# ScalarE's copy of the turned probabilities is moved ahead of the exponential in the even steps of a two-layer attention kernel

## The reference, cut to what matters

```
x   = x + attention0(queries = layernorm(x), keys = values = ctx)   # causal, 16 heads of 64
x   = x + ffn0(layernorm(x))             # gate and up 128 -> 352, down; inputs and weights rounded to FP4
x   = x + attention1(layernorm(x), ctx)  # two softmaxes: 77 text keys, 51 image keys, summed
out = x + moe1(layernorm(x))             # router, 2 of 8 experts, 128 -> 512 -> 128
# attention, per head: softmax(q k^T / 8) v, heads joined, times Wo
```

## Time and profile before

| | |
|---|---|
| median of 3 runs | 696.55 us (695.96 to 699.38) |
| the profiled execution, its own time | 694.58 us |
| its span, first to last instruction | 692.8 us |
| granted TensorE clock, mean | 0.984 |
| busy: TensorE matmul / VectorE / ScalarE / GpSimd | 625.9 / 530.0 / 439.0 / 296.2 us |

### The profile page before, as it was taken

How to read it: one execution, slowest core, us unless ns; L and a number is a source line. 1 busy time by engine, 2 the same in 40 slices (tenths; PEclk the granted TensorE clock), 3 DMA queues, 4 the chain that set the end, 5 groups by cost and what they waited for, 6 DMA issues and landing times.

```text
span 692.8 us, 16579 instructions
## 1 busy us (share of the span) xinstructions
PE 625.9 (90%) x5849; PEld 569.7 (82%) x5849; DVE 530.0 (76%) x1454; ACT 439.0 (63%) x1121; POOL 296.2 (43%) x428
## 2 busy tenths in 40 slices
PE   3779999999899989999999999999999998979980
PEld 2668888888888878999998989988988887979980
DVE  7896677788898888979889898697757675665655
ACT  3668787877777686556565655556656555656660
POOL 3143444334434343353434343334328565565550
PEclk9999999999999999999999999999999999999995
DMA  9700000000000000206666122000000001212215
GB/s 230 229 0 2 1 3 1 1 3 1 1 2 1 1 18 1 89 35 123 124 123 124 29 78 75 2 1 1 3 1 28 28 25 44 62 55 63 73 52 185
DMA packets 49389, 33.27 MB, mean 48 GB/s; under 512 B 9414, under 2 KB 45868, under 8 KB 49308
## 3 DMA queue, kind: packets, MB, share of 16 engines
q1 hardware_dynamic: 47036, 27.55, 16.7%
q0 software_dynamic: 2272, 4.67, 2.0%
HBM read 17.57 MB, written 14.63 MB: 46 GB/s over the span
## 4 chain that ended last, share of the span: by engine, by line
PE 54%; DVE 15%; issue 12%; ACT 9%; POOL 7%; DMA 2%; another core or an unknown queue 0%; POOLq 0%; SPq 0%; ACTq 0%; DVEq 0%
PE ps_s L569 6%; PE ps_j L402 6%; PE ps_h L641 5%; PE ph L1472 5%; PE ps_t L605 5%; PE ps_j L364 4%; ACT scores L782 4%; PE ps_h L620 4%; PE py L1483 4%; PE ps_j L366 4%; PE ps_j L365 3%; DVE scores L1047 3%; POOL probs L1309 3%; POOL xs_scratch L1401 3%; DVE neg_max L1054 2%
## 5 line engine op out<-in xcount | busy, mean ns | idle before, releaser
L1309 POOL TENSOR_TENSOR probs<-scores,rsums 128x308 f32<-128x308 f32 (+1 forms) x192 | 152.8, 810 | 229.6 <-DVE rsums L1067 228.6
L1062 DVE TENSOR_REDUCE sums<-scores 128x4 f32<-128x308 f32 (+1 forms) x192 | 90.8, 500 | 40.1 <-ACT scores L782 34.8
L605 PE MATMUL ps_t<-ident,probs 128*128 128x128 f32 x512 | 78.8, 276 | 21.6 <-ACT probsT L796 18.5
L782 ACT ACTIVATE scores<-scores,neg_max 128x128 f32<-128x128 f32 x256 | 81.6, 393 | 20.2 <-DVE neg_max L1054 19.9
L669 ACT ACTIVATE QT<-ps_j 128x512 f32<-128x512 f32 x64 | 38.3, 598 | 79.6 <-PE ps_j L366 79.5
L605 PEld LDWEIGHTS ps_t<-ident,probs 128*128 128x128 f32 x512 | 57.9, 141 | 28.4 <-issue 23.0
L796 ACT ACTIVATE probsT<-ps_t 128x512 f32<-128x512 f32 x128 | 75.3, 589 | 5.8 <-PE ps_t L605 5.8
L569 PE MATMUL ps_s<-KT,QT 64*128 64x128 f32 x1024 | 75.3, 287 | 0.8 <-ACT KT L675 0.8
L620 PE MATMUL ps_h<-probsT,V 128*64 128x128 f32 x1024 | 70.0, 279 | 0.9 <-DVE x_sb L827 0.8
L569 PEld LDWEIGHTS ps_s<-KT,QT 64*128 64x128 f32 x1024 | 63.0, 189 | 8.9 <-issue 2.4
L641 PE MATMUL ps_h<-Wo,headsT 128*128 128x128 f32 x512 | 69.1, 278 | 0.0
(11 more groups left out here) (239 smaller groups left out, 1608.7 us busy)
## 6 DMA issues: line engine op xcount, KB each, us to landing
xs_scratch<-xs SPq DMA_DIRECT2D x8, 1032.0 KB, 8.1
xt<-xs_scratch SPq DMA_DIRECT2D x39, 64.5 KB
w1b<-in_L_ffn_w_dram SPq DMA_DIRECT2D x1, 2048.0 KB, 9.5
big_raw<-in_L_ffn_w_dram SPq DMA_DIRECT2D x8, 256.0 KB, 4.5
ysum<-y_scratch SPq DMA_DIRECT2D x4, 512.0 KB, 5.2
x_sb<-in_x_dram SPq DMA_DIRECT2D x4, 256.0 KB, 3.9
ctx_sb<-in_ctx_dram SPq DMA_DIRECT2D x4, 256.0 KB, 4.7
Wo<-in_L_xattn_Wo_dram SPq DMA_DIRECT2D x2, 512.0 KB, 7.3
```

The lines of the kernel that those rows point to most:

```text
L605: ins = nc.tensor.transpose(ps_pT[:, j * S:(j + 1) * S], probs[s % 2][:, j, :], ident[:, :])
L782: ins = nc.scalar.activation(scores[s % 4][:, j, :], scores[s % 4][:, j, :], ACT.Exp, bias=neg_max[:, s % 4, 0, j:j + 1])
L1062: ins = nc.vector.tensor_reduce(sums[:, p4, i, :], scores[p4][:, :, k0:k1], AX_X, ALU.add)
L1309: ins = nc.gpsimd.tensor_tensor(probs[(s - 1) % 2][:, :, k0:k1], scores[r][:, :, k0:k1], rsums[:, r, i, :].rearrange("p (h a) -> p h a", a ...
```

## The change: what it does

A helper `copy_probs` holds ScalarE's copy of the turned probabilities with its two waits. In even steps below `STEPS` it is now called right behind the copy of the keys, ahead of the exponential. In odd steps, and in all steps from `STEPS` on, it is called where it was. No other engine's code changes.

```diff
+            def copy_probs(n, s, G, first):
+                if (s >= 2 or not first) and s - 2 < STEPS:
+                    act.wait_ge(SS["pT_ready"], n - 1)
+                    wait_pos(act, SS["heads_ready"], G * BLOCKS + (s - 6) // 2 + 1)
+                    nc.scalar.activation(probsT[(s - 2) % 4][:, :, :].rearrange("p h s -> p (h s)"),
+                                         ps_pT[:, :], ACT.Copy).then_inc(SS["pT_copied"], 1)
+
             def step(G, g, s, lay, prev, first=False, last=False, nxt=None, f=None, fd=None):
...
                     if par == 0 and (hb + 1 < BLOCKS or not last):
                         copy_k(m + 1, (hb + 1) % BLOCKS)
+                    if par == 0:
+                        copy_probs(n, s, G, first)
                     if par == 1:
...
                 for u, t in routes(n):
                     route_mid(u, t)
-                if (s >= 2 or not first) and s - 2 < STEPS:
-                    act.wait_ge(SS["pT_ready"], n - 1)
-                    wait_pos(act, SS["heads_ready"], G * BLOCKS + (s - 6) // 2 + 1)
-                    nc.scalar.activation(probsT[(s - 2) % 4][:, :, :].rearrange("p h s -> p (h s)"),
-                                         ps_pT[:, :], ACT.Copy).then_inc(SS["pT_copied"], 1)
+                if s % 2 == 1 or s >= STEPS:
+                    copy_probs(n, s, G, first)
```

## The result

The changed kernel takes 694.46 us (median of 20 runs, 689.90 to 697.74), the kernel before, run beside it, 696.75 us (20 runs, 695.27 to 701.67). The ratio is 0.9955, with a 95% interval of 0.9940 to 0.9969: 3.1 us faster, between 2.2 and 4.2. The median lies 0.5 us above the forecast's own range (688.5 to 694) and inside the wide one (687 to 697). The profiled execution took 691.88 us by its own time (span 690.1, clock 0.985), 2.70 less than that of before.

The account below looks back on a forecast made before the run. TensorE was taken as the bound (90% busy), stalled in layer 0 on ScalarE's probsT copy (18.5 us). 4.3 + 1.0 = 5.3 us off the 696.55 median gave 691.2 us; own range 688.5 to 694, wide range 687 to 697.

Parts of the forecast that it names:

- Plain blocks: Ten layer 0 blocks where ScalarE never idles: period falls from 6.83 to 6.73, 0.10 us each, 1.0 us in all.
- the ring: Plain blocks' closed chain over TensorE: KT, copy, exponential, headsT with release (0.73), L641 to next KT (3.85); 6.73 us.
- Blocks in which the exponential waits: Nine layer 0 blocks where ScalarE waits for VectorE's maxima: 0.48 us gained in each, 4.3 us in all.
- Blocks that give nothing: Seven layer 0 blocks with FFN matmuls ahead of the turning: late exponential covered, loss 0; uncovered 0.66 each, 4.6 us.
- The slower rival: Late even exponential delays VectorE's sums, FFN pieces and maxima in both layers: +3.3 us, 699.9; chance 0.12.
- The first blocks: 28 to 53 us: the 4.28 us wait largely goes, but VectorE is busy, so gain 0; without that cover 4.3.
- Layer 1: From 276 us: exponential about 0.5 later, TensorE full, so 0; far bounds 16 us lost or 2.4 us won.
- The sign that the prediction named for a loss here: Layer 1: VectorE's sums waiting longer on the even exponential, and that stage longer, would mean the slower case holds.
- the absorbed case: VectorE sets the pace from 144 to 276 us, leaving 0 to 2.5 us of gain, about 695.3; chance 0.18.
- the whole stall goes: Layer 0 after the first blocks: if L641 didn't wait for headsT, 14.2 us would go, giving 682.3; chance 0.08.
- the tie at L641: Block at 79 us: headsT permits L641 at 81.98, it starts at 81.96; taken as leaving no room.
- The case in which the change doesn't do what it says: Copy finds the turning unfinished in most blocks, exchanging waits; the 1.0 us goes, leaving 692.2; no separate chance.

## Why the prediction was right, and where it was not

**What bounds the kernel.** Right: the stall of TensorE in layer 0 was real, and it became a wait at L641 (8.0 us, where 8 or more was forecast).

**Plain blocks.** The mechanism held. The period is 6.69, 0.14 less than before, where 0.10 was forecast. In the ring, headsT with its release takes 0.64 and not 0.73 (0.05 from its end to L641, not 0.15), and L641 to the next KT takes 3.91 and not 3.85. TensorE's own work, however, is not 6.64: with headsT out of the way the period is 6.41. The 6.64 was the period less the idle time of one row. But the busy time follows the period: the profile has TensorE busy for 6.64 of 6.83 us in the kernel before, for 6.69 of 6.69 in the changed one, and for 6.41 of 6.41 with headsT first. Part of the wait for headsT hides behind the turning: L641 starts 0.60 after it in the changed kernel and 0.44 after it with headsT first.

**Blocks in which the exponential waits.** Right, to a hundredth for each block. The lead grows in steps of 0.48 (57, 105, 148, 164, 190, 205, 231, 247 and 273 us): nine, as counted, 4.3 us. The plain blocks bring 1.2 where 1.0 was forecast, 5.5 in all for 5.3.

**Blocks that give nothing.** Right: no lead is lost where the turning is late, and the kernel with the old order in these seven blocks wins nothing by it. The slower rival's mechanism (the late exponential holds up VectorE) cost nothing at the lateness of this change, in either layer. With the exponential another 1.0 us later TensorE's wait for silu_h is 2.4 us longer, which may be a trace of it, and 12.6 us are won all the same.

**The first blocks.** Right, the price is nought. The wait of 4.28 at 38.47 has shrunk to 2.00 us at 36.18, and it is GpSimd's now, but the exponential comes at 52.28 where it came at 52.30, as VectorE's queue has it. It is the same in all seven profiles with probsT alone moved: the lead at TensorE's first turning (32.82 us before), ahead of the first early copy, lies between -0.01 and +1.46; at the next turning it is 2.3 better; and at 50 us it is back to within 0.01 of where it was. That the clock dip at 35 to 45 us would be spared is not shown: it is, in both profiles of the changed kernel and in three more, and it isn't in two others with the same code there. It gives nothing either way: the executions with the early copy in layer 0 alone, which has the dip, and with the router half first, which doesn't, both stand at +1.32 at 50 us. By the clock rule that the prediction quoted from the Trainium skill (TensorE: Matmul & The Clock Gate, Part 1: The HAM clock gate), the shorter idle time spares the dip; the trace agrees in five of the seven. The trace doesn't agree at 525 us in the kernel with the router half first: from 515 us to the fall TensorE has one idle time, of 0.41 us, it is busy for 5.00 of 5.00 us in both windows of the fall, and the clock is 0.51 in the second.

**Layer 1: the step that failed.** It was put at 0, for "TensorE is full". It lost 1.5 us at the router, and won 0.27, so 1.2 us net. I asked who waits for the late exponential, and found nobody in a hurry, rightly. But the part on the change names what stands behind the moved copy in ScalarE's queue in layer 0 (the FFN copy, headsT, V) and never asks it for layer 1, where hidT stands there and empties a bank that TensorE needs within 1.1 us. A full TensorE is no cover for such a wait: the waits of 0.48 and 0.85 us cost 0.6 and 0.9. The 1.2 lies well inside the bounds (2.4 won, 16 lost). The sign that the prediction named for a loss here did appear: from 276 to 560 us VectorE's sums wait 5.8 us for the exponential in 9 waits, where it was 4.8 in 5. But that is not what costs: with the router half first these waits are longer still (7.7 us in 10) and nothing is lost at the router.

**From 5.3 to 3.1.** 5.5 in layer 0 and 1.2 lost in layer 1 make 4.3 us by mechanism: 696.75 - 4.3 = 692.5, and the median is 694.46. The measurement has 3.1 (2.2 to 4.2), so 4.3 is just outside. What is still missing (2.0 us of the medians, 1.2 of the ratio) has no cause that the traces show. It isn't between 50 and 531 us, where executions agree. Behind 531 us they don't: from there to the end one execution of the changed kernel loses 1.6 us and the other gains 1.5. I can't show which part is chance and which is a clock that falls more often behind a shorter layer 0. I also subtracted the whole gain from a median from 3 runs, with no share for that noise. The forecast's own range (688.5 to 694) missed the median by 0.5 us; the wide range held it because it allowed for the absorbed case, which didn't happen, so that part was luck. And the difference is under the 0.5% that the prediction wanted for "faster", to which it gave 0.67; with 20 runs it is clear of none.

**The rivals.** That the whole stall goes (14.2 us) was rightly refused for this change. But it was refused as if the tie at L641 were TensorE's limit: with the second copy moved as well, 12.6 of the 14.2 can be had. Absorption by VectorE is refuted: between 142 and 281 us 3.4 us were won. The case in which the change doesn't do what it says (692.2) didn't come either: the plain blocks did give their 1.2 us.

## What to carry to other kernels

When an instruction is moved ahead in an in-order queue, list everything that now stands behind its wait, in each phase of the kernel separately, and for each find the reader that needs it soonest; the thing that the move was about is often not the one that costs. When a wait vanishes and another of the same engine takes its place at once, try whether the two are in series: move the second producer too, in the order in which the consumer asks for them. Here the first alone gave less than half of the pair (5.5 of 12.6 us) and the second alone lost 28. And compare kernels by the lead of matched instructions, stage by stage: it showed 5.50 to 5.52 us in five executions where the times of whole runs scatter by 8. Then time the kernels all the same, as the lead in one stage is not yet the time: of the 5.5 us 3.1 arrived.

## What the runs showed of the hardware

Copies of a PSUM bank of 128x512 on ScalarE last 0.57 to 0.60 us, but follow one another at 0.48 to 0.50 (78.08, 78.57, 79.05 in the block above), so the price of one in a full queue is 0.48, and that is exactly the size of the steps of the lead. Busy time isn't work: one block of the same instructions keeps TensorE busy for 6.69 of 6.69 us in one kernel and for 6.41 of 6.41 in another. TensorE's granted clock fell to 0.51 in a stretch of 5 us in which it was busy throughout, in two of two executions of one kernel, and in six kernels of eleven it fell within 1.8 to 3.1 us behind the start of the same group of sixteen products of 8 columns. The stretch from 50 to 531 us was repeated from execution to execution to a few hundredths of a microsecond where the clock didn't fall in it; the differences between executions of one kernel came from the start, ahead of 33 us, and from behind 531 us.
